# Eight experts in 544 slots each: weights stationary for the up products, groups of 288 and 256 rows, where tiles of 128 rows ran before

## The reference

```python
router_logits = x @ gate_w.T
topk_w, topk_idx = jax.lax.top_k(routing_probs, TOP_K)      # TOP_K = 2
h = jax.nn.silu(jnp.einsum('nf,efh->enh', x, w1)) * jnp.einsum('nf,efh->enh', x, w3)
y = jnp.einsum('enh,ehf->enf', h, w2)
out = jnp.einsum('enf,ne->nf', y, full_w)                   # added to the token
```

## Time and profile before

| what | value |
|---|---|
| median of 3 runs | 848.59 us (847.27 to 849.71) |
| the profiled execution: its time, and the span of its profile | 847.05 us, 845.4 us |
| mean granted TensorE clock | 0.97 of full speed |
| PE busy | 791.5 us, 94% |
| PEld busy | 655.6 us, 78% |
| DVE, ACT, POOL busy | 351.7, 318.6 and 268.8 us |
| the chain that ended last | PE 86%, DVE 7%, DMA 2% |

### The profile page before, as it was taken

One profiled execution on the slowest core, in us unless ns is written; L12 is line 12 of the kernel. 1 busy time (PEld: TensorE's weight loads), 2 busy tenths in 40 slices (PEclk: granted clock), 3 DMA queues, 4 the chain that ended last, 5 costly groups with the idle time before them and its releaser, 6 DMA issues.

```text
span 845.4 us, 13004 instructions
## 1 busy us (share of the span) xinstructions
PE 791.5 (94%) x3764; PEld 655.6 (78%) x3765; DVE 351.7 (42%) x791; ACT 318.6 (38%) x487; POOL 268.8 (32%) x313
## 2 busy tenths in 40 slices
PE   4999999628999999999999999999999999999993
PEld 3777888527888888888888888888888888888882
DVE  5886758685113621172216223511361172244111
ACT  6784755432214512262127125311441262262120
POOL 4346210003233422361216315322341262243311
PEclk9999999659999999999999999999999999999997
DMA  7247678628111811173116513712281164111111
GB/s 237 47 75 138 150 162 175 256 105 326 25 31 34 317 39 25 27 263 95 32 30 201 159 25 88 271 25 37 46 302 37 25 224 136 25 37 25 30 32 25
DMA packets 55873, 91.72 MB, mean 108 GB/s; under 512 B 7344, under 2 KB 40496, under 8 KB 49712
## 3 DMA queue, kind: packets, MB, share of 16 engines
q1 hardware_dynamic: 45728, 71.64, 27.2%
q0 software_dynamic: 9408, 19.42, 12.0%
q10 hardware_dynamic: 720, 0.46, 0.2%
HBM read 64.97 MB, written 18.15 MB: 98 GB/s over the span
## 4 chain that ended last, share of the span: by engine, by line
PE 86%; DVE 7%; DMA 2%; issue 2%; ACT 1%; POOL 0%; POOLq 0%; ACTq 0%; DVEq 0%
PE bank L720 23%; PE bank L718 23%; PE bank L719 23%; PE bank L734 4%; PE bank L631 3%; PE bank L632 3%; PE bank L633 3%; PE bank L712 2%; PE bank L653 1%; DMA xg<-xn_rows,gather_at 1%; DVE bn L782 1%; DVE wc_lo L823 1%; PE bank L671 1%; PE bank L646 1%; DVE mv L791 1%
## 5 line engine op out<-in xcount | busy, mean ns | idle before, releaser
L718 PE MATMUL bank<-w_hi,xT_hi 128*128 128x512 f32 x576 | 229.0, 398 | 4.3 <-DVE xT_lo L1019 4.3
L720 PE MATMUL bank<-w_hi,xT_lo 128*128 128x512 f32 x576 | 225.9, 392 | 0.0
L719 PE MATMUL bank<-w_lo,xT_hi 128*128 128x512 f32 x576 | 225.2, 391 | 0.0
L1042 DVE TENSOR_TENSOR h<-bank,h 128x512 f32<-128x512 f32 x72 | 49.8, 692 | 294.0 <-PE bank L720 293.8
L718 PEld LDWEIGHTS bank<-w_hi,xT_hi 128*128 128x128 f32 x576 | 108.9, 189 | 26.3 <-DVE xT_lo L1019 4.7
L720 PEld LDWEIGHTS bank<-w_hi,xT_lo 128*128 128x128 f32 x576 | 108.7, 189 | 23.4
L719 PEld LDWEIGHTS bank<-w_lo,xT_hi 128*128 128x128 f32 x576 | 108.9, 189 | 21.8
L718 PE MATMUL bank<-w_hi,hT_hi 128*128 128x512 f32 x288 | 118.7, 412 | 0.0
L559 ACT ACTIVATE h<-bank 128x512 f32<-128x512 f32 x72 | 43.1, 599 | 197.4 <-PE bank L720 197.4
L720 PE MATMUL bank<-w_hi,hT_lo 128*128 128x512 f32 x288 | 112.6, 391 | 0.0
L719 PE MATMUL bank<-w_lo,hT_hi 128*128 128x512 f32 x288 | 112.3, 390 | 0.0
(11 more groups left out here) (145 smaller groups left out, 924.2 us busy)
## 6 DMA issues: line engine op xcount, KB each, us to landing
w_raw<-in_units SPq DMA_DIRECT2D x48, 1024.0 KB, 5.9
joint<-xs_parts SPq DMA_DIRECT2D x64, 128.0 KB, 3.8
out_x<-XT SPq DMA_DIRECT2D x17, 256.0 KB, 3.6
XT<-in_x SPq DMA_DIRECT2D x16, 256.0 KB, 7.0
xn_rows<-xnb SPq DMA_DIRECT2D x16, 256.0 KB, 2.5
xg<-xn_rows,gather_at POOLq DMA_INDIRECT x37, 3.4
out_x<-y,add_at POOLq DMA_INDIRECT x36
gate_row<-gate_rows,gate_at POOLq DMA_INDIRECT x36
```

The lines of the kernel that those rows point to most:

```text
L718: pe.matmul(B[bank][:], stat_hi, hi, start=start, stop=False)
L719: pe.matmul(B[bank][:], stat_hi, lo, start=False, stop=False)
L720: return pe.matmul(B[bank][:], stat_lo, hi, start=False, stop=stop)
L1042: dve.tensor_tensor(h[:, j, :], B[2 * j + 1][:], h[:, j, :], ALU.mult).then_inc(h_out, 1)
```

## The change

Work is staged by expert, no more by tile. Each expert gets 544 slots whatever its count: five pieces (table TILE) in two groups. The wide group holds 288 rows (pieces 0, 1 and 2 with 128, 128 and 32 rows), the even group 256 (pieces 3 and 4). Rows over 544 would go through a loop behind the last expert, which is skipped when there are none.

- **Up products** (`up`): now 128 columns of a weight half are stationary and the group's turned rows move, 288 or 256 columns a matmul. A chunk is 128 hidden units: 24 matmuls. A group has 8 chunks. The result comes out turned already, so h is not turned on PE.
- **Down products**: the wide group again with weights stationary (`down_turned`, 4 x 24 matmuls of 288), then three pieces are turned back (`turn_back`) in the even group's chunks 0, 2 and 4. The even group has its rows stationary (`down_rows`, 2 x 24 matmuls of 512).
- **ACT and DVE** work by chunk on 288 or 256 columns, from SBUF tiles hs. ACT copies yT. All low halves of weights are on DVE. At a wide group's chunks 1 and 3 units 4 and 5, in the even group unit 0 after chunk 5, unit 1 after chunk 7 and units 2 and 3 behind that, for the next expert.
- **Tables.** The slot tables, the gates and the table of rows over 544 are made inside the first expert's wide group, where before they stood ahead of the first product. The second count of PE stands ahead of the first slots now.
- **POOL** gathers into two buffers. Each gather of gates goes straight to slot_gate, and each scatter is issued as its y is there.

```diff
+ROOM = 4 * P + P // 4
+WIDE, EVEN = 2 * P + P // 4, 2 * P
+TILE = ((0, 0, 0, P), (1, 0, P, P), (4, 0, 2 * P, P // 4), (2, 1, 0, P), (3, 1, P, P))
...
+            def pool_expert(e, first=False, last=False):
...
+                gather_next(3, 1, 0, 2, 1)
+                gather_next(4, 0, 0, 3, 2)
...
+                if not last:
+                    gather_next(0, 0, 1, 5, 3)
+                    gather_next(1, 1, 1, 5, 4)
+                add(0)
+                if not last:
+                    gather_next(2, 0, 1, 6, 5)
+                for j in range(1, len(TILE)):
+                    add(j)
...
+            def rows_out(j, bank, m, nth, gates, opening=False):
+                act.wait_ge(y_ps, nth + 1)
+                act.wait_ge(gate_land[j], gates)
+                if not opening:
+                    act.wait_ge(y_st, nth * 16)
+                act.activation(y[0:m], B[bank][0:m, :], ACT.Copy, scale=slot_gate[0:m, j:j + 1]).then_inc(y_out, 1)
...
+            def up(c, n, cols, i, split, opening=False):
...
+                if not opening:
+                    pe.wait_ge(h_out, n(c - 1))
+                at_col = slice(P * (c % 4), P * (c % 4) + P)
+                for m in range(2):
+                    k, hidden = c // 4 * 2 + m, B[2 * (c % 2) + m][:, 0:cols]
+                    for a in range(NQ):
+                        x_hi, x_lo = xT_hi[i][:, a, 0:cols], xT_lo[i][:, a, 0:cols]
+                        pe.matmul(hidden, w_hi[k][:, a, at_col], x_hi, start=(a == 0), stop=False)
+                        pe.matmul(hidden, w_lo[k][:, a, at_col], x_hi, start=False, stop=False)
+                        ins = pe.matmul(hidden, w_hi[k][:, a, at_col], x_lo, start=False, stop=(a == NQ - 1))
+                ins.then_inc(up_ps, 1)
...
+                for c in range(HC):
+                    if c == 0:
+                        pe.wait_ge(xT_lo_out, e * 5 + 3)
+                    up(c, wide, WIDE, 0, split, first and c < 2)
+                    if c == 1:
+                        gathered(1, e * 32 + 32, 3)
+                        turn_x(xg[1], 5, P)
...
+                pe.wait_ge(y_out, e * 5 + 3)
+                down_rows(0, 4, even, split)
+                down_rows(P, 6, even, split)
...
+                for c in range(HC):
+                    chunk(c, even, EVEN)
+                    if c in (1, 3, 5) and not last:
+                        x_low_half(c // 2, 5, e * 5 + (6 + c // 2))
+                    if c in (5, 7) and not last:
+                        low_half(dve, e + 1, (c - 5) // 2)
+                if not last:
+                    low_half(dve, e + 1, 2)
+                    low_half(dve, e + 1, 3)
```

More of the change, by code:

```diff
@@ L410, in gather_gates @@
+            def gather_gates(j, index):
+                m = TILE[j][3]
                 pool.indirect_dma_start(
[L411 to L435, removed]
@@ new lines, in gather_gates, with gather_tile @@
+                    out=slot_gate[0:m, j:j + 1], out_offset=None, in_=gate_dram,
+                    in_offset=bass.IndirectOffsetOnAxis(ap=index[0:m], axis=0)).then_inc(gate_land[j], 16)
+            def gather_tile(column, m, buffer, turned, nth):
+                pool.wait_ge(xt_ps, nth)
+                pool.wait_ge(xt_ps, turned)
+                pool.tensor_copy(gather_at[buffer][:], src_i[:, bass.ds(pool.snap(column), 1)]).then_inc(gather_index, 1)
+                pool.wait_ge(src_ready, 1)
+                pool.wait_ge(gather_index, nth)
+                gather(xg[buffer][0:m], gather_at[buffer][0:m, 0:1], xg_in[buffer])
@@ L534, in _ @@
                     wc_high(t + 2)
-            for k in range(3):
+            for k in range(UNITS):
                 high_half(act, 0, k)
[L539 to L572, removed]
-                               ACT.Copy).then_inc(xT_hi_out, 1)
[L574 to L588, removed]
[L589 to L591 removed]
+            def x_high(j, bank, turned):
+                _, i, off, m = TILE[j]
+                act.wait_ge(xt_ps, turned)
+                act.activation(xT_hi[i][:, :, off:off + m], B[bank][:, 0:NQ * m].rearrange("p (q i) -> p q i", q=NQ),
+                               ACT.Copy).then_inc(xT_hi_out, 1)
@@ new lines, in down_waits, with down_rows @@
+            def down_waits(c, n, split):
+                if c % 4 == 0:
+                    pe.wait_ge(lo_ready[4 + c // 4], split)
+                if c == 0:
+                    pe.wait_ge(hT_lo_out, n(HC - 1))
+                if c == HC - 1:
+                    pe.wait_ge(hT_lo_out, n(HC))
+            def down_rows(first, bank, n, split):
+                for c in range(HC):
+                    down_waits(c, n, split)
+                    k, a = 4 + c // 4, c % 4
+                    hi, lo = hT_hi[:, c, first:first + P], hT_lo[:, c, first:first + P]
+                    pe.matmul(B[bank][:], hi, w_hi[k][:, a, :], start=(c == 0), stop=False)
+                    pe.matmul(B[bank][:], hi, w_lo[k][:, a, :], start=False, stop=False)
+                    ins = pe.matmul(B[bank][:], lo, w_hi[k][:, a, :], start=False, stop=(c == HC - 1))
+                ins.then_inc(y_ps, 1)
@@ new lines, in down_turned @@
+            def down_turned(q, n, split):
+                turned, rows = B[6 + q % 2][:, 0:WIDE], slice(P * q, P * q + P)
+                for c in range(HC):
+                    if q == 0:
+                        down_waits(c, n, split)
+                    k, a = 4 + c // 4, c % 4
+                    pe.matmul(turned, w_hi[k][:, a, rows], hT_hi[:, c, :], start=(c == 0), stop=False)
+                    pe.matmul(turned, w_lo[k][:, a, rows], hT_hi[:, c, :], start=False, stop=False)
+                    ins = pe.matmul(turned, w_hi[k][:, a, rows], hT_lo[:, c, :], start=False, stop=(c == HC - 1))
+                ins.then_inc(yT_ps, 1)
@@ new lines, in _ @@
+            pe.wait_ge(src_ready, 2)
+            pe.wait_ge(xg_in[0], 16)
+            turn_x(xg[0], 5, P)
+            pe.wait_ge(xg_in[1], 16)
+            turn_x(xg[1], 4, P)
+            pe.wait_ge(xg_first, 16)
+            turn_x(y_rows, 6, P // 4)
+            pe_expert(0, first=True)
+            with pe.Fori(1, E - 1) as e:
+                pe_expert(e)
+            pe_expert(E - 1, last=True)
+            pe.wait_ge(rest_ready, 1)
+            total = pe.value_load(all_rest[0:1, 0:1], min_val=0, max_val=REST)
@@ new lines, in dve_expert, with wide, even @@
+            def dve_expert(e, first=False, last=False):
+                def wide(c):
+                    return e * 16 + c
+                def even(c):
+                    return e * 16 + (8 + c)
+                for c in range(HC):
+                    chunk(c, wide, WIDE)
+                    if first and c < 2:
+                        low_half(dve, 0, 2 + c)
+                    if c == 1:
+                        x_low_half(3, 5, e * 5 + 4)
+                    if first and c == 2:
+                        gate_shifts()
+                        slot_tables()
+                    if first and c == 3:
+                        make_gates()
+                    if c == 4:
+                        x_low_half(4, 5, e * 5 + 5)
+                    if c in ((4, 5) if first else (1, 3)):
+                        low_half(dve, e, 4 + (c - 4 if first else c // 2))
+                    if first and c == 6:
+                        rest_tables()
+                for c in range(HC):
+                    chunk(c, even, EVEN)
+                    if c in (1, 3, 5) and not last:
+                        x_low_half(c // 2, 5, e * 5 + (6 + c // 2))
+                    if c in (5, 7) and not last:
+                        low_half(dve, e + 1, (c - 5) // 2)
+                if not last:
+                    low_half(dve, e + 1, 2)
+                    low_half(dve, e + 1, 3)
@@ new lines, in _ @@
+            for j, bank in enumerate((5, 4, 6)):
+                x_low_half(j, bank, j + 1)
+            dve_expert(0, first=True)
+            with dve.Fori(1, E - 1) as e:
+                dve_expert(e)
+            dve_expert(E - 1, last=True)
+            dve.wait_ge(rest_ready, 1)
+            everything = dve.value_load(all_rest[0:1, 0:1], min_val=0, max_val=REST)
+            with dve.If_ne(everything.val, 0):
+                with dve.Fori(0, REST) as r:
+                    live = dve.value_load(rest_live[0:1, bass.ds(r, 1)], min_val=0, max_val=1)
+                    with dve.If_ne(live.val, 0):
+                        x_low_half(0, 5, r + (E * len(TILE) + 1))
+                        for k in range(UNITS):
+                            low_half(dve, r + E, k)
+                        for c in range(HC):
+                            chunk(c, lambda k: r * 8 + (16 * E + k), P)
+                        dve.nop()
```

463 lines of the change are left out of this document (275 added, 188 removed).

## The result

The changed kernel takes 901.85 us (median of 4 runs, 899.92 to 906.17); the kernel before, beside it on the same chip, 847.93 us. The ratio is 1.064 with a 95% interval of 1.0595 to 1.0686: slower by 54 us. The forecast was 908 us, with a range of 874 to 936.

What follows compares the result with a forecast made beforehand. PE was taken as bound by how far apart matmuls start. Start 188.5, work 607.2, first expert 2.4 + 5.4, seven boundaries 87.5, end 1.8 + 12.0 make a 904.8 us span, 908 us on the median; range 874 to 936.

Steps and rivals of the forecast that it cites:

- the extra 13.4 ns: Matmul spacing beyond 512 columns at 2.4 GHz; taken as fixed per matmul, giving 133.3 ns for 288 columns, 120.0 for 256.
- The rival by columns: Rival: the spacing's extra time goes with the columns, 127.5 and 113.3 ns; 895 us in all, chance 0.24.
- The loads as bound: Rival: weight loads at their recorded 189 ns set the matmul spacing; 1142 us in all, chance 0.04.
- PE's work: Matmuls and transposes of all eight experts without waits: 607.2 us, a gain of 31 us.
- The hole: At each of seven expert starts, PE waits for gathered rows queued behind piece 4's scatter and gates: 8.6 us (7.0 to 10.4).
- W: Time at which the last expert's PE work ends; waits at the next expert's start are counted from it.
- The clock: At seven boundaries, PE's clock falls to 0.50 after 8.6 us idle, costing 2.4 us each (0 to 2.7).
- The even tail: At each expert's end, down_rows waits for chunk 6's low half: 0.6 us, up to 2.8 if y is held; 1.5 taken.
- E: Time at which an expert's even group starts; the steps at the expert's end are counted from it.
- The first expert: DVE's added work, tables included, holds PE 5.4 us (2 to 9) in the first wide group; cold clock 2.4.
- The end: Last expert: piece 4's y starts 1.8 us behind PE's end, then 12.0 us to the span's end.
- The rival of a hidden gather: Rival: rows land by 6.4 us after the last expert's end, the clock stays up; 831 us, chance 0.06.

Runs made afterwards that it cites:

- Run 4: Changed kernel with each weight transfer of experts 1 to 7 cut to 32 of 512 columns per chunk, same number of transfers: 881.91 us.
- run 1: Changed kernel with POOL gathering rows of the next expert's pieces 3 and 4 right behind piece 2's scatter, not behind piece 4's: 835.33 us.
- run 2: Changed kernel with two y buffers taken in turn by pieces, POOL's order unchanged: 858.90 us.
- run 6: Changed kernel with 48 unread matmuls of 512 columns ahead of PE's wait for gathered rows in experts 1 to 7: 895.77 us.
- run 5: Changed kernel with 26 unread matmuls of 512 columns ahead of PE's wait for gathered rows in experts 1 to 7: 900.75 us.
- run 3: Changed kernel with both the earlier gathers of pieces 3 and 4 and the two y buffers: 816.33 us.
- run 7: Run 3's kernel with the table for rows over 544 made in three parts behind even-group chunks 0, 2 and 4 of the first expert: 813.77 us.

## Why the prediction was right

**The spacing.** The step that took the extra 13.4 ns as fixed for each matmul holds: 133.3 and 119.8 ns against 133.3 and 120.0. The rival by columns had 127.5 and 113.3, which the trace does not have. The loads as bound fall too: 4224 loads with records of 196 ns lie under matmuls 120 to 133 ns apart, and the rule of the Trainium skill's page "TensorE: Matmul & The Clock Gate", Part 3, that a load overlaps only where the row group differs, does not hold here. The same page of the Trainium skill gives N / 2.4 + 2.5 ns (Back-to-back issue gap), 122.5 and 109.2, as the isolated gap of a single matmul; it is not the spacing of this stream. PE's work came to 607.7 us, 607.2 forecast. Two small errors offset each other in it: the 512-column matmuls of down_rows start 0.232 us apart, not 0.2267, which is 2 us in all and whose cause stays open, and a set of transposes took 0.44 us, not 0.47.

**The hole.** Its mechanism was right at each boundary, and its size (8.6 us forecast, 66.7 / 7 = 9.5 measured) came from two errors that offset each other. Piece 3's scatter was taken to land by W + 4, W + 5.8 at the latest; it landed at W + 6.3. The mis-sized term is the landing: 9.34 us, against a free one of 4.7 and 1.6 of allowance for traffic, while its y began at W − 5.25, 0.85 us earlier than forecast. Run 4 shows 3.3 us of the landing to be the weight transfers; another 1.2 go with the issue of 2.82 us beside a low half of DVE, 1.63 in the earlier trace rows., a gather of 8.33 us under loads, was the nearer row, and I used it only as a range. Behind it the chain from y to the landed rows took 9.6 us, not 11.0. Step by step, measured against forecast: y to its index copy 0.84 (1.2), to the scatter 0.99 (0.94), from there to the gates' gather 2.56 (2.87), to the copy of gather_at 1.01 (1.49), to the gather 0.97 (0.94), landing 3.23 (3.6). The largest part is the loop's branch and its registers, for which I had added 0.5 to the 0.99 of the gates' issue: POOL has them done while that issue runs, as these rows in order of time show, where the copy starts as the issue ends.

```profile
371.56 1.01 POOL L424 DMA_INDIRECT slot_gate<-gate_rows,gate_at  x1 [0.76 <-POOL gate_at L450]
372.57 0.20 POOL L432 COPY gather_at<-src_i 128x1 int32 x1
```

Runs 1 and 2 confirm both halves of the chain, since each removes one.

**The clock.** It fell at all seven boundaries, for 2.1 us on the mean against 2.4. That it was PE's idleness run 6 shows.

**The even tail.** This term failed: 1.5 us at each boundary was forecast and only expert 6 shows one, 1.19 us. DVE and PE at the second expert's end:

```profile
346.02 2.31 DVE L274 TENSOR_TENSOR w_lo<-w_raw,w_hi 128x2048 fp32r<-128x2048 f32 x1
348.25 0.41 DVE L1198 TENSOR_TENSOR hs<-bank,hs 128x256 f32<-128x256 f32 x1
349.14 0.43 DVE L1201 TENSOR_TENSOR hT_lo<-hs,hT_hi 128x256 fp32r<-128x256 f32 x1 [0.48 <-ACT hT_hi L595]
```

```profile
349.63 0.50 PE L823 MATMUL bank<-w_hi,hT_hi 128*128 128x512 f32 x1
```

The even group began at 323.87, so the low half ran from E + 22.2 to E + 24.4, as forecast to 0.5 us, and chunk 6's low half was done at 349.57, E + 25.7, in place of E + 26.2. That is when PE wants it. The 0.6 us computed from the rows were an error of 0.5 us in a sum of five steps. The 1.5 that I took in their place was for a y held by the scatter ahead of it. That mechanism is there, but in the first six experts piece 2's y waits only 0.10 to 0.32 us for piece 1's scatter, which costs PE nothing. In expert 6 it waits 1.35 us, and the chain goes on from it over ACT and DVE's low half to PE's wait:

```profile
783.14 0.68 ACT L602 ACTIVATE y<-bank,slot_gate 32x512 f32<-32x512 f32 x1 [1.35 <-DMA out_x<-y,add_at]
```

```profile
790.97 0.50 PE L823 MATMUL bank<-w_hi,hT_hi 128*128 128x512 f32 x1 [0.91 <-DVE hT_lo L1201]
```

The stall of expert 6 is there in runs 1, 4, 5 and 6 too (1.03 to 1.21 us), which have one y buffer, and gone in runs 2, 3 and 7, which have two. So the failed step is the size of this term, 1.5 us at each boundary where 1.19 came once.

**The first expert.** 4.0 us of idle time against 5.4: 1.38 ahead of the down product and 2.62 ahead of its chunk 7. The second is the table, as forecast, 17 instructions from 217.09 to 221.30. What the forecast left out is that the clock falls behind this one too. With that, 7.3 in place of 7.8.

**The end.** Piece 4's y starts at 886.91, 1.5 us behind the last matmul's start, and the span ends 11.8 later (1.8 and 12.0 forecast).

In all, 6.1 us of the forecast weren't there: the tail stall gave back 9.3, the hole took 6.5, and the rest is under 2 us a term. The mechanism was right, but that the sum came within 1% is partly luck, since these two errors, and the two inside the hole, go against each other.

The rival of a hidden gather is what run 1 made true by moving it, and its 831 us stand beside run 1's 835.33. That they are so near is luck too: the rival kept 10.5 us for the even tail, where run 1 had 1.09 of it and 14.3 us behind hs. What I held against this rival, 8 us of issues and landings in the 11.0, is 1.63 + 0.99 + 3.6 = 6.2 us, and 8.1 only with two of the steps from index copy to DMA.

## What to carry to other kernels

A gather for the next stage that stands behind the last scatter of this one, on one in-order queue, costs the whole chain of that scatter; look in the order of the queue, not in its load, which was 26% here. Where removing one wait brings less than it is long, look for the in-order engine behind it: ACT's y held the next expert's silu, and only both edits together brought 85.5 us. And price a landing by the row that lies under the same traffic, not by the free one.

## What the hardware showed beside that

- Columns got dearer as a matmul got narrower: 512 cost 0.443 ns a column in the kernel before (0.453 in the changed one), 288 cost 0.463 and 256 cost 0.468.
- The idle stretches behind which the granted clock was 0.50 on these traces are of 2.60 us and longer (2.60 to 2.73 in the first expert, 2.69 in run 1, 3.9 to 11.0 at boundaries). Those behind which it stayed at 1.00 are 0.8 to 1.95, and one of 2.57 in the kernel before, from 202.47 to 205.04 us. In the first expert a stretch of 1.4 us stands 2.7 us ahead of the one of 2.6, so these rows don't show that length alone decides. The loss behind one varied from 1.25 to 2.65 us between boundaries of one run with nearly the same hole (9.85 and 9.70 us).
- A scatter of 256 KB that adds into rows landed in 4.87 us in the last expert, in 6.15 where it was issued beside a low half of DVE with no weights under way (6.05 with small transfers), and in 9.34 and 9.93 beside a low half and under the weights.
- Dropping fifteen sixteenths of the weights' bytes took 20 us from PE's holes (66.7 to 46.7) and 19.3 from the span. So a DMA share of 0.91 cost here only where a landing stood on PE's path.
